# A graph layer and eight experts on one core: the front on centred halves of x, one more home for weight blocks, and a recursion in pairs of steps

## The chip, the core and the metric

One core of a Trainium2 chip runs the whole program. The metric is the device time of one execution in microseconds, lower is better. TensorE (PE) multiplies, VectorE (DVE), ScalarE (ACT) and GpSimd (POOL) do the rest, and SyncE (SP) issues nearly all transfers from the chip's memory (HBM) to the cores' own memory.

## The reference, cut to what matters

There are 128 nodes of 768 features and 4096 edges. A layer norm is followed by two graph attention convolutions (8 heads of 768 features, then one head), a residual, a second layer norm, and a mixture of 8 experts, of which each node uses one. A small tridiagonal recursion over the nodes turns a dot product of the expert output into two features, which a last projection adds to the result.

```python
h = gat_conv(layernorm(x), src, dst, W1, a_src1, a_dst1, b1, 8, 768)   # W1: 768 x 6144
x = x + gat_conv(elu(h), src, dst, W2, a_src2, a_dst2, b2, 1, 768)     # W2: 6144 x 768
n = layernorm(x)
comb = one_hot(argmax(softmax(n @ Wg + bg))) * top_p
ffn = sum_e comb_e * (gelu(n @ W1_e + b1_e) @ W2_e + b2_e)             # e = 0..7, H = 3072
v = clip(ffn @ Wv + bv, -3, 3)
gr, gi = diagonal of (T - i)^-1, T tridiagonal with diagonal v, off-diagonal 1
x = x + ffn + bk_scale * (clip([gr, gi] * mask) @ Wo + bo)
```

## The kernel before

The program is one long order written by hand for each engine, with semaphores between them. It reads 189.6 MB of weights, and each byte is used once.

**Graph stage.** W1 and W2 of the graph layers are read as 32 halves of 1152 KB (3 x 128 rows of 768 columns). The halves go to a ring of nine slots (`slots`, `RING = 9`). SP issues half n as soon as PE has used half n - 9: PE's semaphore `used` counts the blocks that it has consumed, and SP waits for a count before each load. `head_up(h)` multiplies the turned x (`xT`) by the two halves of head h (L1082), and `head_down(h)` does the same with the ELU outputs and W2 (L1122, the last head L1137). Between them stand `scores`, `turn_weights` and `aggregate` (L1110), the 8 rounds of edge counting (L1159), and `turn_biases` (L1150, L1152), which waits for the small loads (`small_in`).

**The front.** x is loaded first (L332). PE runs a few matmuls of the identity (`stay_warm`, L1052, counts in `WARM`), turns raw x by six transposes (L1044), spreads the row of means by a matmul (L1061), and DVE subtracts that row while it copies each half of `xT` out of PSUM (L635, L638). DVE then subtracts the mean in the other layout (L626) for the variance (L628).

**Small loads.** `load_small` (L330) issues 12 small transfers (biases, the gate's columns, broadcast scalars, `wv_half`) on SP's queue right after half 5 of the ring.

**Experts.** Each of 8 rounds takes 14 blocks: 6 `chunk` blocks of 1536 KB (128 rows of w1, `up(k)`, L1299) and 8 `lower` blocks of 1152 KB (w2, `down(q)`, two blocks each, L1326). A block needs a home in on-chip memory. Round 0 goes to 6 chunks and 8 lowers laid over the graph stage's memory as it falls free. Round 1 has three chunk homes of its own (`extra0` to `extra2`, called `extra` in the trace), and all its other blocks wait until round 0 has consumed a block. From round 2 on each of the 14 homes is refilled when PE has consumed what it held: two homes called `left`, three `extra`, one chunk, and eight lower homes.

**The end.** After the last `down`, DVE forms the last part of the dot product (L942), PE places and turns it (L1400, L1403, L1404), and DVE runs the recursion `cf_w` (L953, L954): 8 steps, each an operation that waits for the one before it, on shrinking rows of 36 to 8 elements. Then come products of 2x2 matrices over chunks, with matmuls between them (L1413, L1422, L1425, L1430), the output rows (L1033, L1035) and the store (L401). PE fills its waits there with `stay_warm(WARM[10])` and `stay_warm(WARM[11])`.

```python
for i in range(CL):                                   # L951 to L955, CL = 8
    n = 4 * (CL + 1 - i)
    step(V.tensor_tensor(cf_t[:, 0:n], cf_w[:, i + 1, 4:4 + n], cf_w[:, i, 0:n], ALU.subtract))
    step(V.scalar_tensor_tensor(out=cf_w[:, i + 2, 0:n], in0=cf_w[:, i + 1, 0:n],
                                scalar=cf_v[:, i:i + 1], in1=cf_t[:, 0:n], op0=ALU.mult, op1=ALU.add))
```

`step` makes DVE wait for the end of the instruction. The ELU of a graph block (`elu(k)`, 16 of them) is an add (L708), a minimum (L710), a maximum (L711), ScalarE's exponential (L504) and a combining operation (L717).

## Time and profile before

| | us |
|---|---|
| median of 3 runs | 497.94 (496.27 to 499.31) |
| the profiled execution, its own time | 497.94 |
| its span, first to last instruction | 496.1 |
| PE busy | 465.3 (94%) |
| DVE busy | 135.7 (27%) |
| ACT busy | 62.0 (13%) |
| transfers | 190.24 MB, 383 GB/s over the span |

The span holds the program's own instructions, and the device time is 1.8 us longer. In a row of the timeline stand start, length, engine, line, operation, tiles; a row that is merged covers several instructions (xN) from the first start to the last end. For SP (SPq) the length is that of the issue alone, and the landing is a number of its own.

### The profile page before, as it was taken

The page shows a single profiled execution, that of the slowest core. Times are in us where ns is not written, and L with a number is a line of the kernel's source. Part 1 is how long each engine was busy: PE and PEld are TensorE (multiplying, and loading weights), DVE is VectorE, ACT ScalarE, POOL GpSimd, SP SyncE. Part 2 cuts the span into 40 slices and gives each one's busy share as a digit, 9 for nine tenths or more (in the row PEclk, how much of TensorE's full clock was granted, in tenths as well). Part 3 has the DMA queues.
Part 4 walks back from the last instruction along what each step waited for, and adds up shares of the span by engine and source line. Part 5 has one row for each costly group of instructions (what it writes and reads, how often), then busy time and mean ns, then how long its engine had stood idle before and what let it go on. Part 6 is the DMA issues. An engine that isn't in the chain of part 4 may idle for free.

```text
span 496.1 us, 5969 instructions
## 1 busy us (share of the span) xinstructions
PE 465.3 (94%) x2304; PEld 232.8 (47%) x2304; DVE 135.7 (27%) x362; ACT 62.0 (13%) x119; POOL 32.9 (7%) x52
## 2 busy tenths in 40 slices
PE   7999999999999999999999999999998789789881
PEld 6566665667557344344344344344343234224350
DVE  6674697427205320010010010010010001001165
ACT  1010212002003130020020020021020020002100
POOL 3242220000100000000121000000000000000000
PEclk9999999999999998999999999999999999999996
DMA  8989999999999799999999999999999999999800
GB/s 292 332 274 403 401 401 414 413 405 409 426 424 412 291 401 398 384 429 418 424 422 423 426 427 425 424 424 424 424 424 427 427 421 425 425 426 424 338 0 32
DMA packets 32542, 190.24 MB, mean 383 GB/s; under 512 B 5423, under 2 KB 5631, under 8 KB 18190
## 3 DMA queue, kind: packets, MB, share of 16 engines
q1 hardware_dynamic: 31694, 189.94, 93.7%
q8 instruction: 10, 0.16, 0.1%
q0 software_dynamic: 544, 0.05, 0.1%
q10 hardware_dynamic: 288, 0.03, 0.0%
q14 instruction: 6, 0.05, 0.0%
HBM read 189.62 MB, written 0.39 MB: 383 GB/s over the span
## 4 chain that ended last, share of the span: by engine, by line
PE 73%; DMA 12%; SPq 6%; DVE 6%; issue 2%; ACT 0%; POOL 0%; DVEq 0%; POOLq 0%
PE ps L1326 19%; PE ps L1299 19%; DMA lower<-in_L_ffn_W 12%; PE ps L1082 11%; PE ps L1122 11%; SPq L340 6%; PE ps L1312 2%; PE ps L1110 2%; PE ps L1258 2%; PE ps L1137 2%; PE ps L1052 1%; PE ps L1388 1%; PE ps L1044 0%; DVE elu_y L708 0%; DVE cf_w L954 0%
## 5 line engine op out<-in xcount | busy, mean ns | idle before, releaser
L1326 PE MATMUL ps<-lower,hidden 128*64 128x384 f32 x372 | 65.2, 499 | 4.9 <-DMA lower<-in_L_ffn_W 4.7
L1082 PE MATMUL ps<-slot,xT 128*128 128x384 f32 x192 | 64.0, 487 | 0.0
L1299 PE MATMUL ps<-extra,gathered 128*64 128x512 f32 x252 | 57.4, 597 | 4.8 <-DMA extra<-in_L_ffn_W 4.8
L1122 PE MATMUL ps<-slot,eluT 128*128 128x384 f32 x168 | 55.3, 486 | 0.0
L900 DVE TENSOR_TENSOR hidden<-ps,b_T 128x384 f32<-128x384 f32 x32 | 16.9, 554 | 122.7 <-PE ps L1312 122.7
L1082 PEld LDWEIGHTS ps<-slot,xT 128*128 128x128 f32 x192 | 35.7, 190 | 22.6
L1326 PEld LDWEIGHTS ps<-lower,hidden 128*64 128x64 f32 x372 | 26.9, 139 | 40.6 <-issue 31.7
L1326 PE MATMUL ps<-lower_on,hidden 128*64 128x384 f32 x252 | 43.7, 492 | 0.0
L1299 PE MATMUL ps<-chunk,gathered 128*64 128x512 f32 x180 | 40.8, 596 | 1.8 <-DMA chunk<-in_L_ffn_W 1.8
L1122 PEld LDWEIGHTS ps<-slot,eluT 128*128 128x128 f32 x168 | 31.5, 190 | 20.7
L1299 PE MATMUL ps<-left,gathered 128*64 128x512 f32 x144 | 33.3, 598 | 3.2 <-DMA left<-in_L_ffn_W 3.1
L909 DVE TENSOR_SCALAR place_top<-slot_no,rank,small 128x128 f32<-128x128 f32 x8 | 2.8, 346 | 120.4 <-PE ps L1369 116.7
L1299 PEld LDWEIGHTS ps<-extra,gathered 128*64 128x64 f32 x252 | 17.0, 137 | 38.9 <-issue 29.7
L1326 PEld LDWEIGHTS ps<-lower_on,hidden 128*64 128x64 f32 x252 | 16.9, 136 | 19.1 <-issue 16.9
L560 ACT ACTIVATE hidden<-hidden 128x384 f32<-128x384 f32 x32 | 16.1, 522 | 69.7 <-DVE hidden L900 69.7
L1326 PE MATMUL ps<-lower_late,hidden 128*64 128x384 f32 x144 | 24.5, 490 | 0.0
L1299 PEld LDWEIGHTS ps<-chunk,gathered 128*64 128x64 f32 x180 | 12.3, 137 | 25.8 <-issue 21.9
L556 ACT COPY upper<-ps 128x512 f32<-128x512 f32 x24 | 14.1, 586 | 62.4 <-PE ps L1299 62.4
L1299 PEld LDWEIGHTS ps<-left,gathered 128*64 128x64 f32 x144 | 9.6, 136 | 23.0 <-issue 17.3
L1312 PEld LDWEIGHTS ps<-ident,upper 128*128 128x128 f32 x96 | 12.7, 199 | 14.9 <-issue 8.4
L674 DVE CUSTOM_DVE_ANT_0 xc<-h_sb,att_rows 128x768 f32<-128x768 f32 x16 | 16.5, 1034 | 9.0 <-issue 5.4
L1052 PE MATMUL ps<-ident 128*128 128x128 f32 x94 | 14.7, 307 | 2.9 <-DVE ident L617 2.9
(307 smaller groups left out, 333.0 us busy)
## 6 DMA issues: line engine op xcount, KB each, us to landing
slot<-in_L_gnn_W SPq DMA_DIRECT2D x31, 1152.0 KB, 15.6
lower<-in_L_ffn_W SPq DMA_DIRECT2D x31, 1152.0 KB, 14.0
extra<-in_L_ffn_W SPq DMA_DIRECT2D x21, 1536.0 KB, 21.5
lower_on<-in_L_ffn_W SPq DMA_DIRECT2D x21, 1152.0 KB, 24.1
chunk<-in_L_ffn_W SPq DMA_DIRECT2D x15, 1536.0 KB, 13.7
left<-in_L_ffn_W SPq DMA_DIRECT2D x12, 1536.0 KB, 23.8
lower_late<-in_L_ffn_W SPq DMA_DIRECT2D x12, 1152.0 KB, 27.0
slot<-in_L_gnn_W SPq DMA_DIRECT2D x3, 384.0 KB, 6.1
```

Source lines behind the costliest of these rows:

```text
L340: sp.dma_start(lower_homes[i - CHUNKS][:, :, :], view).then_inc(landed[i], 16)
L556: S.copy(upper[:, s * BANK:(s + 1) * BANK], ps[:, s, 0:BANK]).then_inc(upper_ready, 1)
L560: S.activation(hidden[:, q, :, :, :], hidden[:, q, :, :, :], ACT.Gelu_apprx_tanh).then_inc(gelu_done, 1)
L674: dot = V.tensor_tensor_reduce(out=xc[:, :], in0=h_sb[:, h, :], in1=att_rows[:, h % 2, j, :], scale=1.0, scalar=0.0, op0=ALU.mult, op1=ALU ...
L900: V.tensor_tensor(hidden[:, q, :, :, :], ps[:, q, 0:HB].rearrange("p (k b j) -> p k b j", k=3, b=2), b1_T[:, bass.ds(r, 1), :] .rearrange( ...
L1052: T.matmul(ps[:, bank, 0:P], ident[:, :], ident[:, :], start=True, stop=True)
L1082: last = T.matmul(ps[:, 2 * (h % 2) + b, 0:HB], xT[:, 3 * half + k, :], slots[n % RING][:, k, b * HB:(b + 1) * HB], start=(n % 2 == 0 and ...
L1110: last = T.matmul(ps[:, 5 + k % 2, j * P:(j + 1) * P], h_sb[:, h, c:c + P], att_T[:, h % GROUP, :], start=True, stop=True)
L1122: last = T.matmul(ps[:, b, 0:HB], elu_part(KT * h + 3 * half + k, 1)[:, 0, :], slots[n % RING][:, k, b * HB:(b + 1) * HB], start=(h == 0 a ...
L1299: last = T.matmul(ps[b * CAP:(b + 1) * CAP, s, 0:BANK], gathered[:, k, :], upper_homes[k][:, at:at + BANK], start=(k == 0), stop=(k == KT ...
L1312: last = T.transpose(ps[:, q, k * P:(k + 1) * P], upper[:, q * HB + k:(q + 1) * HB:3], ident[:, :])
L1326: last = T.matmul(ps[c * CAP:(c + 1) * CAP, 4, 0:HB], hidden[:, q, k, b, :], lower_homes[i][:, k, c * HB:(c + 1) * HB], start=(i == 0 and ...
```

## The change

Three parts are joined.

1. **Front and graph stage.** DVE centres x in two halves (`centre`), PE turns the centred halves and ScalarE copies them out; the mean's matmul, its copy and PE's first turn of raw x go. The warm-up counts change (5 and 0 in place of 3 and 5). `load_small` moves behind half 8 (`n == RING - 1`) and `turn_biases` behind head 3. The two `wv_half` loads become two ScalarE copies late in the program, `bo` becomes one load by GpSimd, and `b2` comes as four loads of 8 rows by 192 columns. The ELU loses its maximum: the combining operation takes a max in place of an add.
2. **Homes.** The memory of `xn`, `ident_b` and `gb1_T` becomes one more home, `lower_extra`, for a round 1 block. Three `left` homes stand over four vacated lower homes (two over three before). So each load of round 1 waits for one block fewer, and those of round 2 likewise. The product with `b2` (`first_ffn`) moves from round 0 to the end of round 1, and its operand is turned four times, at the end of round 0. `x1` is centred in place after the last round.
3. **Recursion.** `cf_w` is advanced two steps at a time by 4x4 matrices `cf_k`, built for all pairs at once. `WARM[10]` goes from 8 to 2.

```diff
-WARM = (3, 5, 2, 8, 2, 0, 1, 3, 2, 0, 8, 12)
+WARM = (5, 0, 2, 8, 2, 0, 1, 3, 2, 0, 2, 12)
...
-        lowers_2nd = lowers_on
-        chunks_on = left + chunks_2nd[0:4]
+        lowers_2nd = [lower_extra] + [nc.alloc_sbuf_tensor_at(f"lower_2nd{i}", [P, 3, D], f32,
+                                                              offset=moe_base + chunk_at[3 + i])
+                                      for i in range(3)] + lowers[0:4]
+        chunks_on = left + chunks_2nd[0:3]
...
-                if n == 5:
+                if n == RING - 1:
                     load_small()
...
+            sp.wait_ge(used, GNN_HALVES)
+            load(1, 1, CHUNKS, second_in, chunks_2nd, lowers_2nd)
             sp.wait_ge(out2_done, 2)
             load(1, 1, 2, second_in, chunks_2nd, lowers_2nd)
-            load_round(1, 1, second_in, chunks_2nd, lowers_2nd, first=3)
-            for i in range(2):
-                sp.wait_ge(used, used_after(1) - 1 + i)
+            for k, i in enumerate((3, 4, 5, 7, 8, 9, 10, 11, 12, 13)):
+                sp.wait_ge(used, used_after(0) + k + 1)
+                load(1, 1, i, second_in, chunks_2nd, lowers_2nd)
+            for i in range(3):
+                sp.wait_ge(used, used_after(0) + 12 + i)
                 load(2, 2, i, moe_in, chunks_on, lowers_on)
...
+            for half, ready in ((0, xT_first), (1, xT_second)):
+                act.wait_ge(xT_done, half + 1)
+                S.copy(xT[:, 3 * half:3 * half + 3, :].rearrange("p k t -> p (k t)"),
+                       ps[:, 5 + half, 0:HB]).then_inc(ready, 1)
...
-                step(V.tensor_scalar(y, y, 0.0, None, ALU.max))
...
-                                       in1=elu_y[:, k % 2, :, :], op0=ALU.add, op1=ALU.add).then_inc(elu_ready, 1)
+                                       in1=elu_y[:, k % 2, :, :], op0=ALU.add, op1=ALU.max).then_inc(elu_ready, 1)
...
-            pe.wait_ge(x_in, 16)
-            turn_x_half(x_sb, 0)
-            turn_x_half(x_sb, 1)
-            stay_warm(1)
-            pe.wait_ge(mean_ready, 1)
-            T.matmul(ps[:, 4, 0:P], col(MEAN).to_broadcast([P, P]), ident[:, :], start=True,
-                     stop=True).then_inc(mean_spread, 1)
+            for half in range(2):
+                pe.wait_ge(xc_ready, half + 1)
+                turn_x_half(xc, half)
...
-                if h == 2:
+                if h == 3:
                     turn_biases()
```

**SP's order at the small loads.** `slot_58` to `slot_66` are the nine slots; before, and then the change:

```order
L354 DMA slot_63<-in_L_gnn_W 128x3x768
L330 DMA gb_rows<-in_L_gnn_b 16x384
L330 DMA b_rows<-in_L_ffn_b 64x384
L330 DMA b_sb<-in_L_ffn_b 8x768
...
L330 DMA gate_w<-in_L_ffn_Wm 128x6x1
...
L330 DMA wv_half<-in_L_ffn_Wv 64x384 x2
L354 DMA slot_64<-in_L_gnn_W 128x3x768
```

```order
L346 DMA slot_63<-in_L_gnn_W 128x3x768
L346 DMA slot_64<-in_L_gnn_W 128x3x768
L346 DMA slot_65<-in_L_gnn_W 128x3x768
L346 DMA slot_66<-in_L_gnn_W 128x3x768
L322 DMA gb_rows<-in_L_gnn_b 16x384
L322 DMA b_rows<-in_L_ffn_b 64x384
L322 DMA b_sb<-in_L_ffn_b 8x192 x4
...
L322 DMA bk_c<-in_L_ffn_bk_scale 128x1
L346 DMA slot_58<-in_L_gnn_W 128x3x768
```

The small loads stand three halves later, two of them are gone and one is four.

**SP's order where round 0's last blocks and round 1's first ones are loaded** (`chunk_67` to `chunk_69` and `lower_73` on are round 0's homes, refilled):

```order
L340 DMA lower_80<-in_L_ffn_W 128x2304
L335 DMA extra_139<-in_L_ffn_W 128x3072
L335 DMA chunk_67<-in_L_ffn_W 128x3072
L335 DMA chunk_68<-in_L_ffn_W 128x3072
L335 DMA chunk_69<-in_L_ffn_W 128x3072
L340 DMA lower_on_81<-in_L_ffn_W 128x2304
```

```order
L332 DMA lower_80<-in_L_ffn_W 128x2304
L332 DMA lower_extra<-in_L_ffn_W 128x2304
L327 DMA extra_144<-in_L_ffn_W 128x3072
L327 DMA chunk_67<-in_L_ffn_W 128x3072
L327 DMA chunk_68<-in_L_ffn_W 128x3072
L327 DMA chunk_69<-in_L_ffn_W 128x3072
L332 DMA lower_2nd_145<-in_L_ffn_W 128x2304
```

One block of round 1 has moved ahead of the first that must wait for round 0.

**DVE's recursion in the change** (before, it is L953 and L954 eight times in turn):

```order
L948 TENSOR_SCALAR cf_v<-ps 48x8
L951 TENSOR_TENSOR cf_h<-cf_v 48x4
L952 COPY cf_k<-cf_v 48x4x2
L953 TENSOR_SCALAR cf_k<-cf_v 48x4x2
L954 TENSOR_TENSOR cf_k<-cf_v 48x4
L955 SCALAR_TENSOR_TENSOR cf_k<-cf_v 48x4
L957 TENSOR_SCALAR cf_k<-cf_h 48x4x2
L961 TENSOR_TENSOR cf_t<-cf_k 48x64
L967 COPY cf_w<-cf_k 48x16
L969 TENSOR_REDUCE cf_w<-cf_t 48x16
L961 TENSOR_TENSOR cf_t<-cf_k,cf_w 48x64
L969 TENSOR_REDUCE cf_w<-cf_t 48x16
```

The last two rows come once more. Sixteen operations that each wait for the one before have become 13, of which four follow on without a wait.

## Rows read from the trace of the kernel before

**Rows 1.** The page: GB/s in 40 slices of 12.4 us.

```profile
GB/s 292 332 274 403 401 401 414 413 405 409 426 424 412 291 401 398 384 429 418 424 422 423 426 427 425 424 424 424 424 424 427 427 421 425 425 426 424 338 0 32
```

**Rows 2.** Stretches: length, busy us per engine, PE's granted clock, DMA share, GB/s.

```profile
22.00:30.00 8.00, 8.00 (x33) 4.86 (x32) 7.24 (x9) 0.90 (x1) 2.72 (x2) 1.00 0.60 100
30.00:160.00 130.00, 128.77 (x533) 83.87 (x532) 66.87 (x148) 18.82 (x34) 16.75 (x16) 1.00 1.02 410
160.00:168.00 8.00, 8.00 (x46) 3.81 (x46) 0.91 (x5) 2.28 (x6) 0.00 (x0) 1.00 0.60 229
172.00:196.00 24.00, 23.85 (x125) 11.00 (x123) 5.24 (x15) 4.19 (x9) 0.00 (x0) 0.93 0.99 408
196.00:204.00 8.00, 8.00 (x48) 3.33 (x46) 0.45 (x2) 0.48 (x1) 0.00 (x0) 0.98 0.90 315
204.00:468.00 264.00, 250.13 (x1349) 101.58 (x1345) 23.95 (x52) 32.10 (x63) 6.49 (x19) 1.00 1.01 424
```

**Rows 3.** The chain that ended last, its pieces at the end: start, length, what.

```profile
439.82 30.96 DMA lower<-in_L_ffn_W
470.82 2.18 PE ps L1326 x12
```

**Rows 4.** Timeline of SP, four of the small loads, the first and the last of them.

```profile
8.63 3.83 SPq L330 DMA_DIRECT2D gb_rows<-in_L_gnn_b  x1
...
13.09 0.48 SPq L330 DMA_DIRECT2D b_sb<-in_L_ffn_b  x1
14.34 5.04 SPq L330 DMA_DIRECT2D gate_w<-in_L_ffn_Wm  x1
...
25.68 1.13 SPq L330 DMA_DIRECT2D wv_half<-in_L_ffn_Wv  x2
```

**Rows 5.** Timeline of the front, the mean and the first half on PE.

```profile
4.90 0.21 DVE L621 TENSOR_SCALAR small<-small 128x1 f32<-128x1 f32 x1
...
8.59 7.91 PE L1082 MATMUL ps<-slot,xT 128*128 128x384 f32 x24
```

**Rows 6.** PE's groups, 2.9 to 8.5 us: busy, mean ns of one, idle before.

```profile
L1044 PE MATMUL ps<-ident,x_sb 128*128 128x128 f32 x6 | 1.5, 421 | 0.0
```

**Rows 7.** Timeline of the end, ScalarE's copy of 384 columns out of PSUM.

```profile
473.70 0.48 ACT L582 COPY y_sb<-ps 128x384 f32<-128x384 f32 x1 [8.97 <-DVE small L942]
```

**Rows 8.** Issues in 2.62 to 2.70 us: size, us to landing.

```profile
slot<-in_L_gnn_W SPq DMA_DIRECT2D x1, 1152.0 KB, 9.0
```

**Rows 9.** PE's waits up to 205 us: us in total, times, longest.

```profile
PE ps L1110 <- DVE elu_e L710: 0.8, 1, 0.8
```

**Rows 10.** Timeline of SP, 142 to 206 us.

```profile
155.83 0.33 SPq L335 DMA_DIRECT2D extra<-in_L_ffn_W  x1
163.92 7.13 SPq L335 DMA_DIRECT2D chunk<-in_L_ffn_W  x3
```

**Rows 11.** The last stretch, after PE's granted clock fell; columns as in rows 2.

```profile
486.40:496.00 9.60, 0.92 (x7) 0.68 (x6) 5.31 (x22) 0.00 (x0) 0.00 (x0) 0.50 0.10 41
```

**Rows 12.** Timeline of DVE in the end: recursion's first and last, and like operations.

```profile
474.99 0.19 DVE L953 TENSOR_TENSOR cf_t<-cf_w 48x36 f32<-48x36 f32 x1
...
478.81 0.42 DVE L957 TENSOR_TENSOR cf_m<-cf_w,own_chunk 48x256 f32<-48x256 f32 x1
...
486.46 0.22 DVE L997 TENSOR_TENSOR cf_p<-ps,own_chunk 48x64 f32<-48x64 f32 x1 [0.40 <-PE ps L1422]
486.71 0.26 DVE L999 TENSOR_REDUCE cf_b<-cf_p 48x4 f32<-48x64 f32 x1
...
487.89 0.16 DVE L1009 TENSOR_REDUCE cf_r<-cf_q 48x8 f32<-48x16 f32 x1
487.97 0.15 DVE L1010 TENSOR_REDUCE cf_a<-cf_q 48x8 f32<-48x16 f32 x1
```

**Rows 13.** Timeline of PE in the end: the `bo` row and the fills.

```profile
479.80 1.55 PE L1416 MATMUL ps<-b_sb,bk_c 1*128 1x384 f32 x4
481.28 2.94 PE L1052 MATMUL ps<-ident 128*128 128x128 f32 x24
```

More of the change, by code:

```diff
@@ L137, in gnn_moe_kernel @@
               ("cf_f", [P, CL, 2]), ("cf_pre", [2, GC, GC, 4, 4]), ("cf_px", [2, GC, 4, 2, 4]),
-              ("cf_sx", [2, GC, GC - 1, 4, 4])]
+              ("cf_sx", [2, GC, GC - 1, 4, 4]), ("cf_k", [CP, CL // 2, 16]), ("cf_h", [CP, CL // 2])]
         (cf_w, cf_v, cf_t, cf_m, cf_mm, cf_s, cf_x, cf_n, cf_p, cf_b, cf_y, cf_th, cf_q, cf_r, cf_a,
-         cf_d, cf_c, cf_g, cf_e, cf_f, cf_pre, cf_px, cf_sx) = [place(*t) for t in tail_tiles]
-        assert top[0] <= moe_base + lower_at[4] + slot
+         cf_d, cf_c, cf_g, cf_e, cf_f, cf_pre, cf_px, cf_sx, cf_k, cf_h) = [place(*t) for t in tail_tiles]
+        assert top[0] <= moe_base + lower_at[1] + 3 * slot
         top[0] = after_moe
@@ L189, in gnn_moe_kernel @@
         bk_c = place("bk_c", [P, 1])
-        minus_bk = place("minus_bk", [P, 1])
-        half_pow = place("half_pow", [P, 1])
         alpha = place("alpha", [P, 2, HEADS])
-        alpha2 = place("alpha2", [P, 2, 2])
         small = place("small", [P, 64])
+        minus_bk, half_pow, keep, part_f, ones = (small[:, i:i + 1] for i in range(45, 50))
+        logit = small[:, 50:51 + EXPERTS]
+        alpha2 = small[:, 60:64].rearrange("p (a b) -> p a b", a=2)
+        more = place("more", [P, EXPERTS + 12])
+        rank = more[:, 0:EXPERTS + 2]
+        shifted = more[:, EXPERTS + 2:EXPERTS + 6]
+        direction = more[0:CP, EXPERTS + 6:EXPERTS + 8]
+        route_f, feats = more[:, EXPERTS + 8:EXPERTS + 10], more[:, EXPERTS + 10:EXPERTS + 12]
+        whole = place("whole", [P, 8], i32)
+        part_i, route, shifted_i = whole[:, 0:1], whole[:, 1:3], whole[:, 3:7]
         e8 = place("e8", [P, EXPERTS])
-        logit = place("logit", [P, EXPERTS + 1])
         prob = place("prob", [P, EXPERTS])
@@ L591, in _ @@
             S.activation(wo_rows[:, 0, :], wo_rows[:, 0, :], ACT.Identity, scale=bk_c[:, :]).then_inc(rows_scaled, 1)
+            act.wait_ge(end_spread, 2)
+            S.copy(wv_half[0:CAP, :], wv_row[0:CAP, 0:HB])
+            S.copy(wv_half[CAP:P, :], wv_row[CAP:P, HB:D]).then_inc(wv_ready, 1)
             act.wait_ge(last_dot, 1)
@@ L614, in _ @@
             V.tensor_scalar(e8[:, :], free_f[:, 0:EXPERTS], -float(EXPERTS), None, ALU.add)
-            for copy in range(2):
-                V.tensor_scalar(slot_no[:, copy, :], free_f[:, 0:CAP], 1.0, None, ALU.add)
             V.tensor_scalar(ident[:, :], free_f[:, :], part_f[:, :], None, ALU.is_equal).then_inc(consts, 1)
@@ L1275, in first_ffn @@
                 pe.wait_ge(hot_T_ready, 1)
-                for b in range(2):
-                    T.matmul(ps[:, 6 + b, 0:HB], hot_T[:, :], b2_sb[0:EXPERTS, b * HB:(b + 1) * HB],
-                             start=True, stop=True)
+                for n, g in enumerate((0, 2, 1, 3)):
+                    own = slice(g * ROW_GROUP, g * ROW_GROUP + EXPERTS)
+                    at = g % 2 * (HB // 2)
+                    T.matmul(ps[:, 6 + g // 2, at:at + HB // 2], hot_T[own, :], b2_sb[own, :], start=False, stop=True,
+                             skip_group_check=True).then_inc(b2_added, 1)
+                    if n % 2:
+                        pe.wait_ge(b2_added, n + 1)
             def round_(r, first=False, second=False):
@@ L1352, in round_ @@
                     down(1)
-                    T.matmul(ps[0:EXPERTS, 7, 0:P], hot_top[:, :], ident[:, :], start=True,
-                             stop=True).then_inc(hot_turned, 1)
                     pe.wait_ge(place_ready, 2)
@@ L1357, in round_ @@
                     gather(5)
-                    first_ffn()
                     down(2)
                     down(3)
-                    T.matmul(ps[:, 3, HB:HB + 1], ones[0:1, :], top16[0:1, KEEP - 1:KEEP], start=True,
+                    T.matmul(ps[:, 3, HB:HB + 1], ones[0:1, :].to_broadcast([1, P]), top16[0:1, KEEP - 1:KEEP], start=True,
                              stop=True).then_inc(thr_done, 1)
+                    for g in range(4):
+                        last = T.matmul(ps[g * ROW_GROUP:(g + 1) * ROW_GROUP, 7, 0:P], hot_top[:, :], ident[:, :],
+                                        start=True, stop=True)
+                    last.then_inc(hot_turned, 1)
                     return
@@ L1365, in round_ @@
                 up(0)
-                scatter(r)
+                scatter(r, second)
                 up(1)
@@ L1396, in _ @@
             round_(1, second=True)
+            first_ffn()
             with pe.Fori(2, rounds) as r:
@@ L1414, in _ @@
                      start=True, stop=True).then_inc(cf_moved, 1)
+            pe.wait_ge(end_rows_in, 64)
             for b in range(2):
[L1416 to L1417 removed]
+                last = T.matmul(ps[:, 6 + b, 0:HB], bk_c[0:1, 0:1].to_broadcast([1, P]),
+                                bo_row[0:1, b * HB:(b + 1) * HB], start=False, stop=True,
                                 skip_group_check=True)
```

168 lines of the change are left out of this document (83 added, 85 removed).

## The prediction

> **What bounds the kernel now.** I read the page's GB/s line first [rows 1]. It stands at 400 to 427 nearly everywhere, with three weak places: the first three slices, slice 14 (161 to 174 us) and slice 17. PE is busy too, but from 204 us on it has 14 us to spare in 264, while the transfers have none: share 1.01 at 424 GB/s [rows 2]. The chain says the same from the other side. It ends in a transfer that lay 30.96 us in the queue and landed at 470.8, then one block's 2.18 us on PE [rows 3], then 23 us of small serial steps. So the time is the length of the stream of transfers plus the tail, and a gain must come from a hole in the stream or from the tail. That PE or DVE does less elsewhere counts only through the homes that it frees.
>
> The holes, by the stretches [rows 2], against the full rate of 424:
> - 22 to 30 us at 100 GB/s: 8 x (1 - 100/424) = 6.1 us. SP is busy with small loads, one of which holds it for 5.04 us [rows 4].
> - 160 to 168 us at 229 GB/s: 3.7 us. Between the issues at 155.83 and 163.92 there is no home [rows 10].
> - 172 to 196 us at 408 GB/s: 0.9 us. 196 to 204 us at 315 GB/s: 2.1 us.
>
> Between 30 and 160 us the share is 1.02 [rows 2]: the queue never ran dry, so homes were not short there. The 410 GB/s belongs to those transfers.
>
> **The front.** The mean is ready at 5.11 us and PE's first half starts at 8.59 [rows 5]. The change puts between them: a centring of 384 columns, about 0.4; three turns, 0.75 (six took 1.5 us [rows 6]); a ScalarE copy of 384 columns, 0.48 [rows 7]; with the handovers about 1.85. PE starts near 6.95, 1.6 us earlier. But the second half lands at 2.61 + 9.0 = 11.6 us [rows 8], and PE would want it at 6.95 + 3.9 = 10.9. It got it at 12.6 before, so 1.0 us is kept. PE is slow at first (six 128-column rows in 1.5 us [rows 6], 24 in 2.94 in the tail [rows 13]); as long as that lasts no longer than the 8.5 us of before, it eats time only ahead of the same wait. The shorter ELU removes PE's single wait in the graph stage, 0.8 us [rows 9] (DVE drops one operation in each of the five blocks ahead of it). Together PE is **1.8 us earlier** at the end of the graph stage. By itself this is worth nothing to the stream.
>
> **The small loads.** They move behind three more halves, so the hole moves from 22 us to about 31 us and stays. Its length is set by SP's issues: two `wv_half` issues of 1.13 us go, and four `b2` loads replace two. The `b2` issue took 0.48 us [rows 4] and the `bo` issue 0.24, so 4 x 0.48 - 0.72 = 1.2 us come: a draw. The 0.19 MB of `wv_half` are 0.4 us of stream. Taken: **-0.4 us** (bounds +1.2 and -1.5). PE needs half 9 at 45.6 us and the small loads at 40.8; by the shift of three halves (8.8 us) they land near 41.5 and 38, so PE doesn't wait. The loads that they hold up on SP are halves 9 and on, for which PE has these 4 us.
>
> A rule bears on this. The Trainium skill, "DMA: Bandwidth & Descriptors", in its "Rules for kernel authors", wants many small transfers coalesced, since under 64 KB one pays mostly overhead. This trace agrees that the cost is in the issue. By the rule the four `b2` loads of 6 KB are a loss, and the front would be +0.8 us in place of -0.4.
>
> **The homes.** PE frees round 0's first chunk at 163.92 [rows 10]. The extra home lets 1.18 MB follow the last lowers at once, 2.8 us at 424 GB/s, and PE frees the chunk 1.8 us earlier, at 162.1. The hole of 3.7 us is smaller than 2.8 + 1.8 - 0.4, but a new queue needs a moment to fill: **-3.4 us** (bounds -2.8, the block alone, and -3.7). After this each load is released one consumed block earlier, about 2.4 us. The hole at 196 to 204 comes from such releases, but partly from something else: the stretch from 172 to 196 is thin with loads queued. I take two thirds of 2.1: **-1.4 us** (bounds 0 and -3.0, with the stretch before it). `first_ffn` moved behind round 1, the four turns of `hot_top` (1 us) and the centring of `x1` at the end of DVE's last round lie under the stream; with PE's 14 us to spare [rows 2] they cost nothing, and if it had none, the four turns would cost their 1 us.
>
> **The recursion.** Before: 478.81 - 474.99 = 3.82 us for 16 operations that wait, 0.24 each [rows 12]. After: four that follow without a wait at 0.08 to 0.1 (L1009 to L1010), 0.36; two that wait, 0.4 to 0.48; one copy, 0.09; three multiplies of 64 elements at 0.25 (L997 to L999) and three sums at 0.26 and a handover of 0.03, 1.62 [rows 12]. Sum 2.5, so **-1.3 us** (bounds -0.8, if an operation on a four-dimensional view is dearer, and -1.5). The matmul behind it is free at 477.5, since the fill of 8 is now 2. The added waits (`wv_ready`, `end_rows_in`) are met 5 us ahead, under the last four `down` blocks.
>
> **Sum.** 0.4 + 3.4 + 1.4 + 1.3 = 6.5 us. The profiled execution took 497.94, which is the median too. **497.94 - 6.5 = 491.4 us.** About 0.5% (2.5 us) is what a measurement of this kernel can tell from no change.
>
> **The rivals.**
> - *The holes close less.* PE gains nothing in the front (its speed rises later, or the biases come late), and the dent at 196 us isn't a matter of homes. What remains is 0.4 + 2.8 + 1.3 = 4.5: 493.4 us. For it: loads were queued while the stretch from 172 to 196 us was thin. 17%.
> - *They close more.* All of 3.7, 2.1 and 0.9 go, and with nine halves queued the small loads overlap so that the front's hole shrinks by 1 us: 0.4 + 6.7 + 1.0 + 1.3 = 9.4, 488.5 us. 11%.
> - *PE slows in the tail.* PE's granted clock was 0.50, its lower level of 1.2 GHz, from 486.4 us [rows 11], 2.2 us after the fills ended. With six fills fewer it may fall before the `bo` row and the twelve fills, 1.55 and 2.94 us [rows 13]. They would take 9 us from 478.5 and end at 487.5, where the state is ready at 484.7: 2.8 us, and 0.6 for L1413. 491.4 + 3.4 = 494.8, up to 495.5. The Trainium skill, "TensorE: Matmul & The Clock Gate", in "What's actually happening", speaks for it: the slow state is the default and activity releases it. Against it: PE has matmuls until 477.5 and the gap to 478 is short. 10%.
> - *Slower: the small loads jam the queue.* SP spent 18.2 us on their issues, 8.63 to 26.81 [rows 4]. If with nine halves ahead of them they took half as long again, the hole would grow by 9.1 us, half 9 would come at 50.6 us, after PE's 45.6, and the time would be 500.5. It decides from 9 us more (6.5 gained and 2.5), a hole of 15 us. Against it: the first of them met five halves in flight before and meets five again, since SP itself waits for room at each half. 4%, of a bound that the trace doesn't show.
>
> **How the numbers follow.** My forecast has 58%, the rivals 17, 11, 10 and 4. The range takes in the first two rivals and most of the clock's: 488.0 to 495.4. Faster by over 0.5% means under 495.4: 58 + 17 + 11 and a fifth of the clock's, 0.87 with rounding. Within 0.5%: the rest of the clock's case, 0.09. Slower: 0.04.
>
> **What would show it.** Right: the stretch from 160 to 168 us above 400 GB/s; a hole of 5 to 6 us at 31 to 38 us; the first half on PE at about 7 us, a wait for a `slot` transfer of 0.7 us behind it; `used` of the graph stage done 1.8 us earlier; the last block at 465 to 466 us; 2.5 us from the first `cf_h` to `cf_m`. Wrong: two holes in the front; PE waiting on biases at 41 us; a hole that has moved from 160 to before 150 us; a granted clock of 0.50 before 484 us.

## The result, and the profile after

The changed kernel took **490.98 us** at the median (four runs, 489.61 to 492.58), the kernel before beside it 497.69: a ratio of **0.9873, 95% interval 0.9849 to 0.9897**. Six more runs of the changed kernel in the experiments below gave 491.63 and a ratio of 0.9883 [0.9861, 0.9905]; the mean of all ten is 491.3 us, beside 497.2 us for the 46 runs of the kernel before beside the experiments, and the gain is about 6 us.

The profiled execution took 489.61 us with a span of 487.8. Between the profiles of before and after, the last block landed 6.8 us sooner (470.8 to 464.0) and the stretch from there to the landing of the output shrank from 25.0 to 23.4 us. The page's line of GB/s, for [rows 1]:

```profile
GB/s 309 403 261 400 403 400 419 415 400 412 423 426 412 367 398 422 426 425 421 407 418 425 423 427 427 421 425 426 423 423 426 427 423 423 426 427 423 388 1 32
```

Slice 2 rose from 332 to 403, slice 3 fell a little, and slice 14 rose from 291 to 367. In stretches, the columns as in [rows 2]:

```profile
22.00:30.00 8.00, 8.00 (x33) 4.84 (x32) 5.82 (x8) 0.90 (x1) 2.85 (x2) 1.00 1.03 399
30.00:40.00 10.00, 10.00 (x44) 5.99 (x43) 4.20 (x6) 0.90 (x1) 4.69 (x6) 1.00 0.79 230
160.00:168.00 8.00, 8.00 (x42) 3.10 (x38) 1.90 (x14) 1.60 (x2) 0.00 (x0) 1.00 0.87 335
172.00:196.00 24.00, 23.77 (x144) 11.29 (x140) 3.08 (x7) 3.94 (x8) 0.00 (x0) 1.00 1.00 414
196.00:204.00 8.00, 8.00 (x46) 2.85 (x46) 0.45 (x2) 0.75 (x2) 0.00 (x0) 1.00 1.01 430
204.00:460.00 256.00, 244.93 (x1329) 100.60 (x1327) 25.09 (x53) 33.00 (x65) 6.85 (x17) 1.00 1.01 423
```

The front's hole moved to 30 us and is 10 x (1 - 230/424) = 4.6 us long, where it was 6.1. The one at 160 us is 8 x (1 - 335/424) = 1.7 us, where it was 3.7. The one at 196 us is gone. From 204 us on the rate is the same (423 and 424 GB/s). The chain still ends in a transfer and one block on PE, for [rows 3]:

```profile
433.75 30.27 DMA lower<-in_L_ffn_W
464.06 2.18 PE ps L1341 x12
```

SP's small loads, on its timeline, for [rows 4]:

```profile
17.11 2.77 SPq L322 DMA_DIRECT2D gb_rows<-in_L_gnn_b  x1
...
20.79 1.62 SPq L322 DMA_DIRECT2D b_sb<-in_L_ffn_b  x4
...
22.89 4.85 SPq L322 DMA_DIRECT2D gate_w<-in_L_ffn_Wm  x1
...
33.11 18.26 SPq L346 DMA_DIRECT2D slot<-in_L_gnn_W  x10
```

They hold SP for 16.0 us (17.11 to 33.11), where it was 18.2. The `Wm` load is as dear as before. PE's front on its timeline, for [rows 5]:

```profile
5.58 1.25 PE L1059 MATMUL ps<-ident,xc 128*128 128x128 f32 x6 [0.47 <-DVE xc L631]
7.05 8.02 PE L1093 MATMUL ps<-slot,xT 128*128 128x384 f32 x24 [0.22 <-ACT xT L490]
```

SP's issues at the end of the graph stage, for [rows 10]. The first row is where PE reports `used` 32, the last where it frees round 0's first chunk:

```profile
147.57 0.81 SPq L332 DMA_DIRECT2D lower<-in_L_ffn_W  x2
148.43 0.43 SPq L332 DMA_DIRECT2D lower_extra<-in_L_ffn_W  x1
153.41 0.33 SPq L327 DMA_DIRECT2D extra<-in_L_ffn_W  x1
161.50 7.13 SPq L327 DMA_DIRECT2D chunk<-in_L_ffn_W  x3
```

The extra home's load goes out at 148.43 us, right behind the last lowers, and the chunk's at 161.50 in place of 163.92. PE's wait of 0.8 us for the ELU [rows 9] is gone from its list of waits. The recursion on DVE's timeline, for [rows 12]:

```profile
468.23 0.15 DVE L951 TENSOR_TENSOR cf_h<-cf_v 48x4 f32<-48x4 f32 x1
...
470.29 0.21 DVE L969 TENSOR_REDUCE cf_w<-cf_t 48x16 f32<-48x64 f32 x1
470.53 0.42 DVE L972 TENSOR_TENSOR cf_m<-cf_w,own_chunk 48x256 f32<-48x256 f32 x1
```

It takes 470.53 - 468.23 = 2.30 us, where it took 3.82. Last, PE in the tail, for [rows 13]:

```profile
471.52 1.55 PE L1434 MATMUL ps<-bo_row,bk_c 1*128 1x384 f32 x4
473.00 4.58 PE L1067 MATMUL ps<-ident 128*128 128x128 f32 x24
477.83 0.31 PE L1440 MATMUL ps<-cf_s,to_chunks 2*48 2x64 f32 x2 [0.25 <-DVE cf_s L1009]
```

and the stretch in which the fills ran:

```profile
474.10:477.40 3.30, 3.30 (x17) 3.20 (x15) 2.92 (x19) 0.00 (x0) 0.00 (x0) 0.50 0.00 0
```

The granted clock was 0.50, the level of 1.2 GHz, and the 24 fills took 4.58 us instead of 2.94. They ended at 477.58, 0.25 us before the state let L1440 start.

### The profile page after: what moved, and what is told of

Read it like the earlier page. It is cut to its first block, busy times and chain, and to the rows that moved or that the text cites. A ratio compares the mean times of both kernels' runs of the same rounds, so it can differ in the third digit from the quotient of the medians.

```text
span 487.8 us, 5909 instructions
## 1 busy us (share of the span) xinstructions
PE 461.4 (95%) x2292; PEld 230.0 (47%) x2292; DVE 127.0 (26%) x341; ACT 63.8 (13%) x123; POOL 33.4 (7%) x50
## 4 chain that ended last, share of the span: by engine, by line
PE 71%; DMA 14%; SPq 8%; DVE 4%; issue 1%; ACT 0%; DVEq 0%
PE ps L1341 18%; PE ps L1314 17%; PE ps L1093 13%; PE ps L1133 11%; DMA extra<-in_L_ffn_W 7%; DMA lower<-in_L_ffn_W 6%; SPq L332 6%; SPq L327 3%; PE ps L1327 2%; PE ps L1121 2%; PE ps L1269 2%; PE ps L1148 2%; PE ps L1404 1%; DMA x_sb<-in_x 1%; PE ps L1059 0%
## 5 line engine op out<-in xcount | busy, mean ns | idle before, releaser
L1314 PE MATMUL ps<-left,gathered 128*64 128x512 f32 x216 | 49.3, 597 | 3.8 <-DMA left<-in_L_ffn_W 3.3
L1341 PE MATMUL ps<-lower_2nd,hidden 128*64 128x384 f32 x252 | 43.2, 490 | 2.5 <-DMA lower_2nd<-in_L_ffn_W 2.5
L1341 PE MATMUL ps<-lower,hidden 128*64 128x384 f32 x216 | 36.8, 489 | 1.3 <-DMA lower<-in_L_ffn_W 1.0
L1341 PE MATMUL ps<-lower_on,hidden 128*64 128x384 f32 x216 | 37.5, 492 | 0.0
L905 DVE TENSOR_SCALAR place_top<-free_f,more,small 128x128 f32<-128x128 f32 x8 | 3.5, 440 | 119.3 <-PE ps L1385 115.6
L1314 PEld LDWEIGHTS ps<-left,gathered 128*64 128x64 f32 x216 | 14.6, 136 | 34.4 <-issue 26.7
L1341 PEld LDWEIGHTS ps<-lower_2nd,hidden 128*64 128x64 f32 x252 | 17.5, 137 | 24.3 <-issue 19.8
L1341 PEld LDWEIGHTS ps<-lower,hidden 128*64 128x64 f32 x216 | 15.3, 137 | 20.0 <-issue 16.5
L1314 PE MATMUL ps<-chunk,gathered 128*64 128x512 f32 x108 | 24.3, 597 | 0.0
L1327 PE MATMUL ps<-ident,upper 128*128 128x128 f32 x96 | 17.1, 304 | 0.0
```

The source lines that it names most:

```text
L1314: last = T.matmul(ps[b * CAP:(b + 1) * CAP, s, 0:BANK], gathered[:, k, :], upper_homes[k][:, at:at + BANK], start=(k == 0), stop=(k == KT ...
L1327: last = T.transpose(ps[:, q, k * P:(k + 1) * P], upper[:, q * HB + k:(q + 1) * HB:3], ident[:, :])
L1341: last = T.matmul(ps[c * CAP:(c + 1) * CAP, 4, 0:HB], hidden[:, q, k, b, :], lower_homes[i][:, k, c * HB:(c + 1) * HB], start=(i == 0 and ...
```

## The experiments

All were timed beside the kernel before, which stood at 497.0 to 497.2 us. The changed kernel has a mean of 491.3 over ten runs. Single runs of a variant spread over 1 to 4 us, so a difference between the means of two variants is uncertain by about 1.2 us (twice 1.15, the spread of six runs of the changed kernel, times the root of 1/6 + 1/10). What a step is worth is therefore read from the time and from the places in the profile together. The table has both, by the labels of the experiments, the places in microseconds from the span's start: the end of PE's first 24 matmuls, `used` 32 (issue of the first two `lower` loads of round 0's end), the issue of the first freed chunk, and the landing of the last block.

| kernel | runs | median | ratio [95%] | 24 end | used 32 | chunk | last block |
|---|---|---|---|---|---|---|---|
| before | | 497.1 | 1 | 16.50 | 150.00 | 163.92 | 470.8 |
| changed, first profile | 4 | 490.98 | 0.9873 [0.9849, 0.9897] | 15.07 | 147.57 | 161.50 | 464.0 |
| a0_changed | 6 | 491.63 | 0.9883 [0.9861, 0.9905] | 15.75 | 148.25 | 162.17 | 465.7 |
| e1_pairs | 12 | 496.80 | 0.9986 [0.9972, 1.0001] | 16.48 | 150.00 | 163.91 | 471.7 |
| e3_nohome | 6 | 493.67 | 0.9923 [0.9901, 0.9946] | 15.69 | 148.19 | 162.11 | 467.5 |
| e4_late_pe | 5 | 492.89 | 0.9911 [0.9893, 0.9929] | 18.42 | 150.92 | 164.84 | 468.3 |
| e5_oldfront | 4 | 490.87 | 0.9876 [0.9856, 0.9895] | 15.72 | 148.22 | 162.14 | 464.7 |
| e6_act_small | 5 | 492.10 | 0.9891 [0.9872, 0.9911] | 16.81 | 149.31 | 163.22 | 466.5 |
| e7_fill24 | 6 | 492.95 | 0.9916 [0.9890, 0.9943] | 15.26 | 147.76 | 161.68 | 465.1 |
| e8_fill4 | 6 | 491.98 | 0.9889 [0.9868, 0.9910] | 16.26 | 148.77 | 164.34 | 467.5 |
| e9_elu_max | 5 | 492.56 | 0.9896 [0.9876, 0.9915] | 17.32 | 150.83 | 164.74 | 468.6 |
| e10_steps | 6 | 492.85 | 0.9920 [0.9899, 0.9941] | 15.79 | 148.29 | 162.21 | 465.0 |
| e11_early_fill | 5 | 490.99 | 0.9870 [0.9850, 0.9890] | 15.51 | 148.00 | 162.29 | 465.5 |
| e13_old_early | 4 | 490.41 | 0.9871 [0.9847, 0.9895] | 15.67 | 148.17 | 162.08 | 464.7 |

Each row has the places of one profile. Two regularities run through it. From the end of the 24 matmuls to `used` 32 PE takes 132.5 us in each kernel with the new ELU and 133.5 in each with the old. And with the new homes the last block lands 302.5 to 303.9 us after the first freed chunk's load goes out, in every variant; without the extra home 305.4, in the old layout 306.9 and 307.8.

**The changed kernel again**, as the mark for the others.

> The changed kernel again, on the chip and in the rounds of the three beside it, as their yardstick. Both theories: 0.987 of the kernel before, within 0.2%, some 491 us. Its own profile should again show the first free chunk's load issued near 161.5 us and the last block landing near 464 to 466 us.

**Without the extra home.** The load of round 1's seventh block, its first `lower`, goes back to where it was, behind the freed chunks, and each later load of rounds 1 and 2 waits for one more consumed block (the cut shows the first two of four places).

```
-            sp.wait_ge(used, GNN_HALVES)
-            load(1, 1, CHUNKS, second_in, chunks_2nd, lowers_2nd)
...
-            for k, i in enumerate((3, 4, 5, 7, 8, 9, 10, 11, 12, 13)):
+            for k, i in enumerate((3, 4, 5, 6, 7, 8, 9, 10, 11, 12, 13)):
```

> The changed kernel with the home lower_extra left empty until round 0 has consumed a block, and every load of rounds 1 and 2 released one consumed block later, as before the change. Theory A (the stream runs dry at 160 us for want of homes, whatever the front did): the hole between 160 and 168 us grows by the 2.8 us of the missing block, and the one at 196 to 204 us comes back with 1 to 2 us, together 3.8 to 4.8 us slower than the changed kernel. Rival B (the front's shorter hole is what paid, the home only fills what would have been filled anyway): under 1 us slower.

It took 2.0 us more than a0 at the median. Its stretches:

```profile
160.00:168.00 8.00, 8.00 (x42) 3.24 (x40) 1.80 (x14) 1.60 (x2) 0.00 (x0) 1.00 0.62 237
...
196.00:204.00 8.00, 8.00 (x48) 2.69 (x44) 0.45 (x2) 0.74 (x2) 0.00 (x0) 1.00 1.02 430
```

The hole at 160 us is back (3.5 us against a0's 1.4), the one at 196 us is not. The 2.0 us lie between the two theories: theory A is right on the first hole and wrong on the second. So the extra home, with the earlier releases that go with it, is worth about 2 us, and the second hole doesn't need them.

What closed the second hole can be read from PE. In e3 the last `lower` of round 1 waits for the same count of `used` as in the kernel before, yet it goes out at 190.90 us in place of 195.84. PE's lead at `used` 32 is 1.8 us of that. The rest is in PE's rows of the kernel before:

```profile
188.96 0.39 PE L1353 MATMUL ps<-ident,hot_top 128*8 128x128 f32 x2
189.27 1.55 PE L1258 MATMUL ps<-place_now,x 128*128 128x64 f32 x12
190.76 1.55 PE L1277 MATMUL ps<-b_sb,hot_T 8*128 8x384 f32 x4
192.24 9.65 PE L1326 MATMUL ps<-lower,hidden 128*64 128x384 f32 x48
```

```profile
192.80:196.20 3.40, 3.40 (x12) 1.23 (x10) 0.00 (x0) 0.00 (x0) 0.00 (x0) 0.50 1.00 420
```

and in those of e3:

```profile
187.22 1.55 PE L1269 MATMUL ps<-place_now,x 128*128 128x64 f32 x12
188.70 7.96 PE L1341 MATMUL ps<-lower,hidden 128*64 128x384 f32 x48
```

The turn of `hot_top` (L1353) and the product with `b2` (L1277), which the change moves out of this place, held PE for 1.8 us. And PE's granted clock was 0.50 from 192.8 to 196.2 us, so that the 48 matmuls took 9.65 us in place of 7.96; 1.4 us of this came before the release (3.60 us from their start to it, 2.20 in e3). The load then went out only 3.0 us before the one ahead of it landed, and landed 4.4 us after that one in place of 2.8. The profile of e1 below, the only other one with the old order of work, has the clock's fall at the same place and the same dent; in the changed kernel and its variants the clock doesn't fall there, and the stretch stands at 412 GB/s or more. So the dent belongs to the moved product, to PE's lead and to the clock, in shares that no run separates, and not to the number of homes.

**PE later.** `WARM[1]` from 0 to 10, ten calls of fill between the transposes and the first half.

```
-WARM = (5, 0, 2, 8, 2, 0, 1, 3, 2, 0, 2, 12)
+WARM = (5, 10, 2, 8, 2, 0, 1, 3, 2, 0, 2, 12)
```

> The changed kernel with ten more identity matmuls ahead of PE's first half, so that PE is 2.2 to 2.6 us later in the whole graph stage and nothing else changes. Theory A: the first chunk is freed at 163.9 instead of 161.5 us, transfers wait for it, and the kernel is slower by the same 2.2 to 2.6 us. Rival B (PE's lead is hidden under the stream, which is bound by its bytes alone): 0, within 0.5 us. A middle, 0.5 to 1.5 us, would say that transfers were queued for part of it.

In the profile everything behind moved by 2.7 us: the 24 matmuls' end, `used` 32, the chunk's issue, and the last block by 2.6. The time rose by 1.3 us at the median and 1.8 at the mean, under theory A's 2.2 to 2.6 us and clear of rival B. The stretch from 196 to 204 us stood at 427 GB/s with PE's lead gone (but the clock did not fall there either). PE's place in the graph stage reaches the end of the stream: nearly one for one in this profile, for two thirds in the mean time.

**The front as before.** `x` is turned raw, its mean taken off behind the transposes, the small loads go behind slot 5.

```
-                if n == RING - 1:
+                if n == 5:
                     load_small()
...
-            for half in range(2):
-                pe.wait_ge(xc_ready, half + 1)
-                turn_x_half(xc, half)
+            pe.wait_ge(x_in, 16)
+            turn_x_half(x_sb, 0)
+            turn_x_half(x_sb, 1)
+            stay_warm(1)
+            pe.wait_ge(mean_ready, 1)
+            T.matmul(ps[:, 4, 0:P], col(MEAN).to_broadcast([P, P]), ident[:, :], start=True,
+                     stop=True).then_inc(mean_spread, 1)
```

> The changed kernel with the front as before: raw x turned, the mean spread by a matmul, the small loads behind half 5, the biases turned behind head 2, five identity matmuls ahead of the first half; the shorter ELU, homes and recursion stay. Theory A: PE is 1.6 us later at 160 us and the stream 1 to 2 us shorter of blocks, of which the later chunk release decides: 1.5 to 2.5 us slower than the changed kernel, so 4 to 5 us under the kernel before. Rival B (the front's stream gain of 2.7 us counts in full): 2.7 us or more slower.

Both theories missed: it took no longer than the changed kernel (490.87 us). Its stretches and its first half on PE:

```profile
22.00:30.00 8.00, 8.00 (x33) 4.84 (x32) 7.90 (x9) 0.90 (x1) 4.34 (x2) 1.00 0.63 136
...
160.00:168.00 8.00, 8.00 (x42) 3.21 (x40) 1.76 (x14) 1.60 (x2) 0.00 (x0) 1.00 0.93 376
```

```profile
7.71 8.01 PE L1102 MATMUL ps<-slot,xT 128*128 128x384 f32 x24
```

The old hole is back at 22 us, and at 150 us the stream is 1.8 us behind a0's (150.42 against 148.60 for the same load). But a0 then waits for PE's releases and this kernel does not, and the chunk issued at 162 us lands at 168.88 in the one and 168.71 in the other. The first half starts 0.7 us later than a0's (6.99), but more of it runs at the higher clock, so its end is the same: 15.72 against 15.75. Against the kernel before it starts 0.9 us sooner although the front's order is the same, since the identity is ready 0.3 us sooner (the table of slot numbers is gone ahead of it) and the granted clock rose sooner in this run.

After these four the theory was: a hole in the stream ahead of 148 us costs nothing, because the stream waits there for PE; the end is set by when PE frees homes and by how many there are. The next runs test it.

**The recursion alone**, in the kernel before.

```
-            for i in range(CL):
-                n = 4 * (CL + 1 - i)
-                step(V.tensor_tensor(cf_t[:, 0:n], cf_w[:, i + 1, 4:4 + n], cf_w[:, i, 0:n], ALU.subtract))
...
+            for i in range(1, CL // 2):
...
+                step(V.reduce_sum(flat[:, 16 * (i + 1):16 * (i + 2)],
+                                  cf_t[:, :, :, :].rearrange("p o c k -> p (o c) k"), AX))
```

> The kernel before with the third part of the change alone: the recursion in pairs of steps (and the two matmuls of fill ahead of the state that go with it); homes, front and ELU are as before. Theory A, the recursion stands alone on the path: DVE's stretch from the clamped angles to cf_m goes from 3.8 us to 2.3 us and the whole time falls by 1.5 us, to 495.7 us, ratio 0.997. The last block lands where it landed before, at 470.8 us by the profile. Rival B, the recursion's saving is taken back by the wait for cf_init or by PE's fills: 497.2 us, ratio 1.000.

It gained 0.3 us at the median (ratio 0.9986 [0.9972, 1.0001]), which excludes neither no gain nor one of 1.4. In its profile the stretch behind the last block was 1.5 us shorter, but the last block landed 1.0 us later, with no edit that acts ahead of it. The time alone didn't settle the size. One reason may lie in the fall of the clock at 193 us, which lowers a run's mean granted clock by 0.003: 8 of the 12 runs of e1 stand at 0.987 or below (the profiled one is at 0.987), but only 3 of the 17 of the kernel before beside it. Among the runs above 0.987 the means are 495.7 and 497.1 us, 1.3 us apart. These are few runs, and e10 is the same question from the other side.

**The small loads on ACT's queue**, so that SP issues slots without a pause.

```
-                if n == RING - 1:
-                    load_small()
...
+                    act.dma_start(target, view).then_inc(small_in, 16)
...
                        ps[:, 5 + half, 0:HB]).then_inc(ready, 1)
+            load_small()
```

> The changed kernel with one edit: the small loads (Wm, the gate's weights, biases, wv_half and the others) go out on ACT's queue behind its copies of xT instead of SP's behind the last ring slot, so SP is free to issue the slots. The changed kernel stood at 491.6 us beside this kernel of before. Theory A, the stream's place from 164 us on is set by PE's releases and by the number of homes: the hole at 30 to 36 us goes, slot 9 lands some 3 us sooner (36 us instead of 38.9), but the loads at 148 to 163 us wait for PE's releases all the same and the time stays within 0.5 us, 491.1 to 492.1. Rival B, a hole of the front is lost to the end: 3 us less, 488.0 to 489.0 us. Rival C, ACT is held by its queue while it issues and PE's ELU chain or its gathers come later: PE's used 32 comes after 149 us and the time is 492.5 us or more.

```profile
22.00:30.00 8.00, 8.00 (x33) 4.86 (x32) 6.79 (x9) 0.90 (x1) 2.58 (x2) 1.00 1.06 375
30.00:40.00 10.00, 10.00 (x39) 6.01 (x38) 4.50 (x8) 0.90 (x1) 5.69 (x6) 1.00 1.04 395
146.00:156.00 10.00, 9.54 (x53) 6.72 (x52) 5.79 (x21) 2.69 (x7) 0.00 (x0) 1.00 0.96 385
```

The front's hole is gone: 395 GB/s from 30 to 40 us in place of 230. Half 19 came at 67.36 us, 2.6 us sooner than a0's, while half 9, the first behind the small loads' place, came only 0.7 us sooner (38.14), short of the 3 expected. The time was 492.10 us, half a microsecond over the changed kernel and within its uncertainty: theory A. The lead was lost before 156 us, where the stream met PE's releases (385 GB/s in the last row, 391 in a0, 425 in the kernel before). Rival B's 3 us are excluded. `used` 32 came at 149.31, later than 149 as rival C had it, but not through ACT: PE's 24 matmuls already ended 1.1 us later than a0's, because the clock rose late (below).

**Twice the fills in the tail**: `WARM[11]` from 12 to 24.

> The changed kernel with 24 instead of 12 calls of fill between the two matmuls that follow the state's product, so 24 more instructions on PE. Theory A, PE's fills end just where the state comes (477.6 against 477.8 us in the profile, at the lower clock of 1.2 GHz): each further one is on the path, 24 by 0.12 to 0.19 us is 2.9 to 4.6 us, so 494.3 to 496.2 us, 2.7 to 4.6 us more than the changed kernel. Rival B, PE has slack there that the inferred waits don't show: no more than 0.5 us.

```profile
474.12 7.24 PE L1067 MATMUL ps<-ident 128*128 128x128 f32 x48
481.29 0.31 PE L1440 MATMUL ps<-cf_s,to_chunks 2*48 2x64 f32 x2
```

The state was ready at 478.9 us, and L1440 started at 481.29, behind the fills: the tail was 2.3 us longer (25.8 against 23.4) and the mean time 1.7 us. The sign is theory A's, the size under its range, because the clock came back to 1.0 at 477.5 us and the later fills ran at 0.12 us each. With 12 calls, PE stands just ahead of the state when the clock is low, and 1.9 us ahead when it is not.

**A third of the fills**: `WARM[11]` from 12 to 4.

> The changed kernel with 4 instead of 12 calls of fill between the two matmuls behind the state's product. Theory A, PE ends its fills before the state comes, in runs where the granted clock has fallen in the tail too: no change, 491.0 to 491.6 us. Rival B, in part of the runs the fills at 1.2 GHz are late: 0.3 to 0.8 us less, 490.5 to 491.0 us. Rival C, the fills hold the clock up for the matmuls behind them: 0.5 us more or worse, 491.8 us.

There is no gain: 491.98 us, against rival B. The figure lies over theory A's range and in rival C's, but within the uncertainty of no change, and in the tail there is little for C: the clock was 0.50 from 476.9 us to the end, and the stretch behind the last block took 23.6 us against 23.4. PE now waits 3.04 us there for the state. The profile showed something else, in the middle:

```profile
159.50:162.80 3.30, 3.30 (x10) 1.36 (x11) 0.09 (x1) 0.68 (x4) 0.00 (x0) 0.50 0.91 385
```

```profile
164.34 0.33 SPq L327 DMA_DIRECT2D chunk<-in_L_ffn_W  x1
```

The granted clock was 0.50 for 3.3 us while PE was busy without a pause. It freed the first chunk 15.57 us after `used` 32 instead of 13.92, and the last block landed 1.9 us later than a0's. The edit cannot be the cause, since it acts only from 476 us on; the kernel before has such a stretch at 193 us (e3).

**The ELU as before**, a separate maximum over `y`.

```
                 V.tensor_scalar(e, y, 0.0, None, ALU.min).then_inc(elu_in, 1)
+                step(V.tensor_scalar(y, y, 0.0, None, ALU.max))
```

> The changed kernel with the ELU as before: the separate maximum over y is back and the last step adds, instead of one step that takes the maximum. Same result. Theory A, PE waits at the eight attention blocks' ends for ELU: PE's used 32 comes 0.8 us later (148.4 us), the first chunk's load goes out 0.8 us later, and the last block lands 0.6 to 0.8 us later: 492.2 to 492.5 us. Rival B, with DVE's constants gone and the stream filled by homes, PE's lead brings nothing at the end: within 0.3 us of the changed kernel, 491.3 to 491.9 us.

```profile
PE ps L1122 <- DVE elu_e L708: 0.8, 1, 0.8
```

```profile
6.97 10.35 PE L1094 MATMUL ps<-slot,xT 128*128 128x384 f32 x24
```

The wait is back, and with it 1.0 us between the 24 matmuls and `used` 32 (133.5 us against 132.5). The median rose by 0.9 us and the mean by 1.1, just inside the uncertainty of 1.2: the places say theory A, the time alone doesn't exclude rival B. In the profiled run `used` 32 was 2.6 us later than a0's; 1.6 of that came from the clock's late rise, not from the edit.

**The recursion step by step** in the changed kernel, with its eight calls of fill: the diff of e1 the other way round.

> The changed kernel with the recursion step by step, as in the kernel before (and its eight calls of fill ahead of the state). Same result. The changed kernel stands at 491.3 us over ten runs. Theory A, the recursion stands alone on the path and its 1.5 us in the trace are 1.5 us of the time: 492.8 us, and the stretch from the last block's landing to the end of the output is 1.5 us longer than the changed kernel's 23.5 to 23.8 us. Rival B, what the half kernel with this part alone suggests (0.3 us at the median, 0.7 us at the mean): part of the 1.5 us comes back before the last block lands, 491.6 to 492.0 us, though the stretch behind the last block is longer by 1.5 us.

```profile
469.21 0.19 DVE L950 TENSOR_TENSOR cf_t<-cf_w 48x36 f32<-48x36 f32 x1
...
473.01 0.42 DVE L954 TENSOR_TENSOR cf_m<-cf_w,own_chunk 48x256 f32<-48x256 f32 x1
```

The stretch is 3.80 us again, the tail 24.9 us against 23.4, and the time 492.85 us, 1.7 us over the changed kernel at the mean: theory A, and rival B's range is missed. With e1 (0.3 at the median, 0.6 at the mean) the two timings bracket the 1.5 us of the trace; the tail is shorter by 1.5 us in both pairs of profiles.

**Four calls of fill before PE's first one.**

```
+            V.memset(fill[:, :], 1.0).then_inc(fill_in, 1)
             dve.wait_ge(iota_done, 2)
...
+            pe.wait_ge(fill_in, 1)
+            for _ in range(4):
+                T.matmul(ps[:, 7, 0:P], fill[:, :], fill[:, :], start=True, stop=True)
             pe.wait_ge(consts, 1)
```

> The changed kernel with four calls of fill on PE before its first one, from a tile that VectorE sets to 1 in its first instruction; they end about when the identity is ready, at 2.6 us. In ten profiles the granted clock rose from 1.2 to 2.4 GHz between 6.4 and 11.7 us, and PE's used 32 came between 147.6 and 149.3 us (0.4 us later for each microsecond of a later rise). Theory A, the rise follows PE's activity: it comes sooner on the mean, PE's lead and with it the loads at 148 to 163 us come up to 1 us sooner, 490.3 to 491.1 us. Rival B, the rise is drawn by something else: no change, 491.1 to 491.6 us, and used 32 still lies on the line of rise against lead (147.6 us for 6.4, 149.3 us for 10.7).

```profile
7.05 8.46 PE L1097 MATMUL ps<-slot,xT 128*128 128x384 f32 x24
```

490.99 us, mean 0.5 us under the changed kernel: at the edge of theory A's range, within the uncertainty of no change, and not settled. The rise came at 7.2 us, inside the spread of the others; one profile cannot tell whether it comes sooner on the mean.

**The old front and the early fills together.**

> The kernel with the old front (x turned raw, its mean taken off behind the transposes, small loads behind slot 5), the new homes, recursion and ELU, and the four early calls of fill on PE: the two variants that stood lowest, 490.9 and 491.0 us, joined. Theory A, both lower figures are PE's start and clock and not the variant's own: they do not add, and it stands with them, 490.4 to 491.2 us, within 0.5 us of the changed kernel's 491.3. Rival B, they add: the early fills give PE up to 1 us more lead on a front that costs the stream nothing by 164 us, 489.8 to 490.3 us.

490.41 us, the lowest median of all, as theory A had it. Its ratio, 0.9871 [0.9847, 0.9895], is the changed kernel's within the interval: no version here is shown to beat it.

## Why the prediction was right, step by step

The forecast was 491.4 us by a sum of 6.5, and the medians fell by 6.7. The bound was read rightly: the stream and the tail. The terms inside the sum fared unequally, and that they add up so well is in part luck: one hole closed less than forecast, another closed fully, in part for reasons that the forecast had at nothing. Two of its own signs failed: the stretch from 160 to 168 us stood at 335 GB/s and not above 400, and the clock was at 0.50 at 474 us, before 484.

- **The front's term of 0.4 us** was small for the right reason (a draw of issues) and it is worth nothing at the end. The hole even shrank by 1.5 us, since all the small issues together took 16.0 us and not 18.2, and the stream stood 2.7 us ahead at the last lower; of that, e5 and e6 show that none reaches the end. The step that failed is the sentence that homes were not short between 30 and 160 us because the queue never ran dry there. That held for the stream of before. A stream 2 to 3 us ahead meets `used` 32 at 148 us with too little queued. The rule that the prediction weighed, that many small transfers should be coalesced into one large one, is from the Trainium skill, "DMA: Bandwidth & Descriptors", "Rules for kernel authors". The trace agrees with it: the four `b2` loads held SP for 1.62 us, where one for `b2` and one for `bo` had taken 0.72. At the end it changes nothing either, for the same reason.
- **PE 1.8 us earlier** was right for a0 (150.00 - 148.25 = 1.75); the first profile showed 2.4. The ELU's part is 1.0 and not 0.8, since the old order cost 133.5 against 132.5 us. The start's part is 0.75 in a0 and 1.4 in the first profile, by the moment at which the clock rose. The wait for the second half of the first load, forecast at 0.7 us, was 0.4 to 0.5 and only where the clock rose early.
- **The homes at 160 us, 3.4 us**, was too large for the hole, which went from 3.7 to 1.7 us. The forecast had all but 0.3 closed. In fact the freed chunk's load went out at 161.50, only 1.8 us before the one ahead of it landed (163.32), and landed 5.3 us after that one instead of 3.7. The term was made of the home's block and of PE's 1.8 us. By e3 the home is worth 2.0 us, and by e4 a lead of 1.8 us is worth 1.2 to 1.8 (two thirds of it in the mean time, all of it in the profile). Together that is about the forecast's figure, though this hole alone doesn't show it.
- **The dent at 196 us, 1.4 us**, was too small and had the wrong cause: all of its 2.1 us went. The prediction had releases one block earlier close part of it; e3 has the old releases and 430 GB/s there. It priced the move of `first_ffn` at nothing, but the product and the turn had held PE for 1.8 us just ahead of the release that counts, and the clock's fall of [rows 2] (0.93 from 172 to 196 us) had held it for some 1.4 more. The 0.9 us between 172 and 196 us partly stayed (414 GB/s where it was 408).
- **The recursion, 1.3 us**, was 1.5 in the trace (2.30 us for the forecast 2.5), and 1.7 and 0.6 in the two timed pairs.
- **The rivals.** The clock in the tail did what that rival said: 0.50 from 474.0 us, before the fills were through. Its price was wrong. It had the `bo` row and the fills take 9 us, all at the lower clock, against 6.2 us until the state. But the clock fell only behind the `bo` row and rose again at the fills' end: the two took 6.1 us (471.52 to 477.58), and the state let L1440 start 6.3 us after their start. Twelve calls just fit, and e7 shows that more would not. The jam of small loads didn't come.

By places, a0 against the kernel before: the chunk's release is 1.8 us earlier, the stretch from there to the last block 3.4 us shorter (306.9 to 303.5), of which e3 gives 1.9 to the home and leaves 1.5 for the dent, and the tail is 1.5 us shorter. That is 6.6 us, the difference of the two profiles, against some 6 measured. The dent's part may not be in every run: the mean granted clock stands at 0.987 or below, as in the profile with the fall, in 12 of the 46 runs of the kernel before, whose mean time is 497.8 us, and the other 34 have a mean of 497.0. What lies between is within the uncertainty of the timings and isn't assigned further.

## What to carry to other kernels

A hole in a saturated stream is worth its length only if nothing further on makes the stream wait for a consumer: before counting it, find the next place where a load is issued only just ahead of the queue's end, and ask who frees its buffer. In this kernel the consumer's start was worth more than the loader's pauses (2.7 us of delay cost 1.8, a hole of 4.6 us cost nothing), even while the consumer seemed to have time to spare, and one more buffer at the release that comes last about as much (2 us). Work of the consumer that stands just ahead of a release counts too, and before a hole is put down to the code, look at the clock ahead of it. And filler work on an engine should be sized by the time until the next real operand at the lower clock.
